# Turning the rows of eight experts in the DMA engines, as 16-bit halves, in place of TensorE

## The reference

```python
scores = jax.nn.softmax(xt @ gate_w.T, axis=-1)
topv, topi = jax.lax.top_k(scores, K)                      # K = 4 of E = 8
topv = topv / jnp.sum(topv, axis=-1, keepdims=True)
g = _silu(jnp.einsum('td,edh->eth', xt, exp_w1))
u = jnp.einsum('td,edh->eth', xt, exp_w3)
yexp = jnp.einsum('eth,ehd->etd', g * u, exp_w2)
routed = jnp.einsum('te,etd->td', combine, yexp)
shared = _silu(xt @ sh_w1) * (xt @ sh_w3) @ sh_w2          # 2048 wide
```

## Time and profile before

| | |
|---|---|
| median of 3 runs | 1568.19 us (1567.37 to 1569.07) |
| the profiled execution, its own time | 1567.0 us |
| its span | 1565.3 us |
| mean granted TensorE clock | 0.999 |
| TensorE busy | 1551.4 us, 99% |
| VectorE busy | 854.2 us, 55% |
| ScalarE busy | 584.7 us, 37% |
| moved by DMA | 205.64 MB, mean 131 GB/s |

### The profile page before, as it was taken

The page is one execution under the profiler, slowest core; times in us unless marked ns, Lnnn a source line. Parts: engine busy times, 40 slices in busy tenths (PEclk is TensorE's granted clock), DMA queues, the critical chain, the costliest instruction groups (busy, mean ns, idle before and its releaser), DMA issues.

```text
span 1565.3 us, 28095 instructions
## 1 busy us (share of the span) xinstructions
PE 1551.4 (99%) x10796; PEld 1534.7 (98%) x10796; DVE 854.2 (55%) x1460; ACT 584.7 (37%) x914; POOL 117.8 (8%) x139
## 2 busy tenths in 40 slices
PE   9999999999999999999999999999999999999998
PEld 9998999999999999999999999999999999999998
DVE  8665569845522344454544545454555366335886
ACT  6332345432222333343444444444444222223442
POOL 1321010000100001000010100001000133001000
PEclk9999999999999999999999999999999999999999
DMA  4412203232422446446464654646555576221333
GB/s 136 133 41 72 76 28 108 82 131 84 123 76 79 157 138 189 151 135 208 137 207 148 191 165 150 202 151 208 161 172 163 160 204 178 83 80 55 94 117 83
DMA packets 71001, 205.64 MB, mean 131 GB/s; under 512 B 13620, under 2 KB 22370, under 8 KB 70890
## 3 DMA queue, kind: packets, MB, share of 16 engines
q1 hardware_dynamic: 45020, 157.94, 32.6%
q0 software_dynamic: 14976, 32.81, 7.0%
q10 hardware_dynamic: 10894, 13.26, 2.7%
HBM read 185.01 MB, written 18.95 MB: 130 GB/s over the span
## 4 chain that ended last, share of the span: by engine, by line
PE 94%; DVE 4%; issue 1%; ACT 1%; ACTq 0%; DVEq 0%; POOL 0%; POOLq 0%
PE acc L1793 86%; PE acc L1773 2%; PE acc L2172 1%; PE acc L2151 1%; DVE w_lo L1277 1%; DVE yrow L1042 0%; PE acc L1842 0%; DVE yrow L1041 0%; ACTq L1000 0%; PE acc L2108 0%; PE acc L1758 0%; PE acc L2225 0%; PE acc L1784 0%; PE acc L1952 0%; DVE acc L1323 0%
## 5 line engine op out<-in xcount | busy, mean ns | idle before, releaser
L1793 PE MATMUL acc<-act_x,w_hi 128*128 128x312 f32 (+8 forms) x2304 | 507.6, 309 | 1.6 <-DVE act_b L1290 0.6
L1793 PE MATMUL acc<-act_b,w_hi 128*128 128x312 f32 (+8 forms) x2048 | 456.0, 311 | 0.0
L1793 PE MATMUL acc<-act_a,w_hi 128*128 128x314 f32 (+1 forms) x1920 | 423.0, 310 | 2.7 <-DVE gath L1349 2.3
L1793 PEld LDWEIGHTS acc<-act_x,w_hi 128*128 128x128 f32 x2304 | 385.3, 188 | 2.5 <-ACT act_a L826 1.0
L1793 PE MATMUL acc<-act_x,w_lo 128*128 128x312 f32 (+8 forms) x1152 | 355.7, 309 | 0.0
L1793 PEld LDWEIGHTS acc<-act_b,w_hi 128*128 128x128 f32 x2048 | 340.2, 189 | 0.1
L1226 DVE TENSOR_TENSOR w_lo<-raw,w_hi 128x1024 fp32r<-128x1024 f32 x253 | 309.0, 1222 | 44.2 <-ACT w_hi L502 43.2
L1793 PEld LDWEIGHTS acc<-act_a,w_hi 128*128 128x128 f32 x1920 | 319.5, 190 | 4.0 <-ACT w_hi L798 2.8
L1793 PE MATMUL acc<-act_b,w_lo 128*128 128x314 f32 (+8 forms) x1024 | 315.6, 308 | 0.0
L1793 PE MATMUL acc<-act_a,w_lo 128*128 128x314 f32 (+1 forms) x960 | 294.9, 307 | 0.0
L502 ACT ACTIVATE w_hi<-raw 128x1024 fp32r<-128x1024 f32 x264 | 277.1, 1051 | 8.3 <-PE acc L1793 4.6
(11 more groups left out here) (239 smaller groups left out, 1247.0 us busy)
## 6 DMA issues: line engine op xcount, KB each, us to landing
raw<-stream_dram SPq DMA_DIRECT2D x296, 512.0 KB, 3.7
y_dram<-yrow POOLq DMA_DIRECT2D x16, 512.0 KB
y_dram<-yrow POOLq DMA_DIRECT2D x8, 352.0 KB
rows<-x_dram ACTq DMA_DIRECT2D x1, 2500.0 KB
x_dram<-rows ACTq DMA_DIRECT2D x5, 500.0 KB
h_rows_dram<-rows ACTq DMA_DIRECT2D x1, 2500.0 KB
rows<-x_dram ACTq DMA_DIRECT2D x8, 312.5 KB
rows<-x_dram SPq DMA_DIRECT2D x5, 448.0 KB
```

What stands on the lines that cost most here:

```text
L1793: ins = pe.matmul(o, w, xs_[h], start=(first and w is hi and xs_ is x_hi), stop=(last and w is lo))
```

## The change

Both turns go from TensorE to the DMA engines, by transposing transfers of 16-bit values. A float32 value is kept as two halves of 16 bits in two separate planes (t = 0 and 1), and each plane is turned by itself. Copies on ScalarE and VectorE take words apart into planes and put planes together to words; they move bits only.

- `h_rows_dram` and `y_dram` hold rows of 2 x 1024 halves. `h_rows` (ScalarE) writes the planes as it copies from PSUM.
- **In:** GpSimd gathers one tile at a time (for the first expert all three, into `rows`); SP turns it by one transposing transfer (`turn_inputs`, three for each expert: 128, 128 and 96 rows of 2048 halves) into `xe_parts`. For experts 1 to 7 the three go through one buffer, `x_stage`: SP issues the turn n of expert r+1 behind the load of unit 11, 15 or 19 of expert r, and GpSimd gathers the next tile when the turn before it has landed. VectorE puts the words of chunk m together in `x32` (`expert_in_word`), in the place where it had copied to `yrow`; the high and low parts are taken from there.
- **Out:** ScalarE copies chunk m from PSUM as planes to `y16` (688 halves in place of 344 words); SP turns it by one transposing transfer (`turn_outputs`, eight for each expert, 128 rows of 768 halves) to `yrow`, ahead of the load of unit m of the next expert (or of `shb`); GpSimd stores when all eight have landed. `y16` has two buffers: the copy of chunk m waits until the turn of chunk m-2 has landed.
- **Back:** the gathered rows land as planes in `act_x`, and ScalarE puts the words together (`back_rows`, 20 copies of 2048 halves), behind each of the first five pairs of `shb`, before VectorE adds them.
- TensorE's functions `expert_in` and `turn_y` are gone, and with them the waits that they held; VectorE's first words of an expert wait for the last up unit, whose inputs they may not overwrite.

The core of the diff (the way for more than 344 tokens in an expert changes likewise):

```diff
-            def gather(e):
+            def gather_list(e):
                 pool.tensor_copy(now_tok[:, :], slot_tok[:, bass.ds(3 * e, 3)]).then_inc(now_ready, 1)
                 pool.wait_ge(h_saved, 16)
                 pool.wait_ge(now_ready, e + 1)
                 pool.sem_inc(gather_go, 1)
-                for n, (c0, cn) in enumerate(SLOT_TILES):
-                    pool.indirect_dma_start(out=grow[0:cn, n, :], out_offset=None, in_=h_rows_dram,
...
+            def gather_rest(e):
+                for n in range(1, 3):
+                    pool.wait_ge(xe_turned, e * (16 * 3) + 16 * n)
+                    pool.sem_inc(gather_go, 1)
+                    gather_tile(x_stage, n)
...
             with pool.Fori(1, EXPERTS - 1) as e:
+                pool.wait_ge(x32_ready, e * KC + KC)
+                gather_list(e + 1)
+                gather_tile(x_stage, 0)
                 save_y(e - 1)
-                pool.wait_ge(xe_tp, e * KC + KC)
-                gather(e + 1)
+                gather_rest(e + 1)
...
+            def turn_inputs(e, n, source, count):
+                c0, cn = X_TILES[n]
+                sp.wait_ge(gathered, 16 * count)
+                if e >= 1 and n == 0:
+                    sp.wait_ge(x32_ready, e * KC)
+                sp.dma_start_transpose(xe_parts[:, :, c0:c0 + cn], source[0:cn, :]).then_inc(xe_turned, 16)
+
+            def turn_outputs(e, m):
+                sp.wait_ge(yt_copied, e * KC + m + 1)
+                if e >= 1 and m == 0:
+                    sp.wait_ge(y_saved, 16 * 3 * e)
+                sp.dma_start_transpose(y_parts[:, :, m * P:(m + 1) * P],
+                                       y16[:, m % 2, :, :].rearrange("p t w -> p (t w)")).then_inc(y_turned[m % 2], 16)
...
+            for r in range(EXPERTS):
+                expert = sp.value_load(order_i[0:1, r:r + 1], min_val=0, max_val=EXPERTS - 1)
+                for j in range(UNITS_EXPERT):
+                    if r >= 1 and j < KC:
+                        turn_outputs(r - 1, j)
+                    load_one(r * UNITS_EXPERT + U_EXP + j, j % RING, expert * UNITS_EXPERT + U_EXP + j)
+                    if j in X_TURNS and r + 1 < EXPERTS:
+                        n = X_TURNS.index(j)
+                        turn_inputs(r + 1, n, x_stage, 3 * (r + 1) + n + 1)
+            for j in range(KC):
+                turn_outputs(EXPERTS - 1, j)
+                load_one(U_SHB + j, j % RING, U_SHB + j)
...
                 for m in range(KC):
                     split_hi(base, UNITS_UP + m + 3)
+                    if nxt:
+                        expert_in_hi(e + 1, m)
                     act.wait_ge(unit_done, base + (UNITS_UP + m + 1))
                     if m >= 2:
-                        act.wait_ge(y_tp, e * KC + (m - 1))
-                    act.activation(prod[:, m % 2, 0:CAP], acc[:, m % 4, 0:CAP], ACT.Copy).then_inc(yt_copied, 1)
-                    if nxt:
-                        expert_in_hi(e + 1, m)
+                        act.wait_ge(y_turned[m % 2], e * (8 * KC) + 16 * (m // 2))
+                    act.activation(y16[:, m % 2, :, 0:CAP],
+                                   acc[:, m % 4, 0:CAP].bitcast(u16).rearrange("p (s t) -> p t s", t=2),
+                                   ACT.Copy).then_inc(yt_copied, 1)
...
+            def back_rows(i):
+                for k in range(TOP):
+                    act.wait_ge(back[k], 16 * (i + 1))
+                    if i >= 1:
+                        act.wait_ge(back_used, TOP * (i - 1) + k + 1)
+                    act.activation(back_slot(k).bitcast(u16).rearrange("p (d t) -> p t d", t=2),
+                                   back_parts[0:TT, k, :, :], ACT.Copy).then_inc(back_words, 1)
+
             for m in range(KC):
                 gated_pair(shb, m, b_hi, None)
+                if m < NT:
+                    back_rows(m)
...
+            def expert_in_word(e, m):
+                if m == 0:
+                    dve.wait_ge(xe_turned, e * (16 * 3) + 16 * 3)
+                if m >= 2:
+                    dve.wait_ge(xe_lo, e * KC + (m - 1))
+                dve.tensor_copy(x32[:, m % 2, :].bitcast(u16).rearrange("p (s t) -> p t s", t=2),
+                                xe_halves[:, :, m, 0:CAP]).then_inc(x32_ready, 1)
...
-                    if m >= 1:
-                        turn_y(e, m - 1)
-                    if nxt:
-                        expert_in(e + 1, m)
```

More of the change, by code:

```diff
@@ L25 @@
 SLOT_TILES = [(0, P), (P, P), (2 * P, CAP - 2 * P)]
+XR = 352
+YC = 3 * P
+X_TILES = [(0, P), (P, P), (2 * P, XR - 2 * P)]
+X_TURNS = (11, 15, 19)
 RING = 4
@@ L81, in build @@
         w_lo = sb("w_lo", [P, RING, D], f32r)
-        silu = sb("silu", [P, TP], f32)
-        prod = sb("prod", [P, 2, TP], f32)
+        work = sb("work", [P, 3 * TP], f32)
         ident = sb("ident", [P, P], f32)
@@ L120, in build @@
         now_tok = sb("now_tok", [P, 3], u32)
+        silu = work[:, 0:TP]
+        prod = work[:, TP:3 * TP].rearrange("p (s w) -> p s w", w=TP)
+        e_silu = work[:, 0:CAP]
+        x32 = work[:, CAP:3 * CAP].rearrange("p (s w) -> p s w", w=CAP)
+        y16 = work[:, 3 * CAP:3 * CAP + 2 * YC].bitcast(u16).rearrange("p (s t w) -> p s t w", s=2, t=2)
+        e_prod = work[:, 3 * CAP:3 * CAP + 2 * YC].rearrange("p (s w) -> p s w", w=YC)
         acc = ctx.enter_context(nc.psum_tensor("acc", [P, 8, 512], f32))
@@ L356, in build @@
         yt_copied = sem("yt_copied")
-        y_tp = sem("y_tp")
-        y_copied = sem("y_copied")
+        y_turned = [sem(f"y_turned{s}") for s in range(2)]
         y_saved = sem("y_saved")
         back = [sem(f"back{s}") for s in range(TOP)]
+        back_words = sem("back_words")
         back_used = sem("back_used")
@@ L440, in _, with load_one @@
             sp.dma_start(bias[:, :, :], biases).then_inc(small_loaded, 16)
+            def load_one(done, s, u):
+                sp.wait_ge(hi_split, done + (1 - RING))
+                sp.wait_ge(lo_split, done + (1 - RING))
+                sp.dma_start(raw[:, s, :], stream[bass.ds(u, 1), :, :].rearrange("u p n -> (u p) n")
+                             ).then_inc(raw_loaded[s], 16)
             def load_four(done, first):
                 for s in range(RING):
[L444 to L448, removed]
+                    load_one(done + s, s, first + s)
             def load_seven(L):
@@ L472, in _ @@
+            for n in range(3):
+                turn_inputs(0, n, rows16[:, n, :, :].rearrange("p t d -> p (t d)"), 3)
+            with sp.Fori((U_SHA + UNITS_UP) // RING, U_EXP // RING) as g:
                 load_four(g * RING, g * RING)
             sp.wait_ge(order_ready, 1)
[L474 to L477, removed]
@@ L1588, in expert @@
                     dve.wait_ge(exp.silu, e * KC + (m + 1))
-                    dve.tensor_tensor(prod[:, m % 2, 0:CAP], acc[:, (2 * m + 1) % 4, 0:CAP], silu[:, 0:CAP],
+                    if prev and m < 2:
+                        dve.wait_ge(y_turned[m], e * (8 * KC))
+                    dve.tensor_tensor(e_prod[:, m % 2, 0:CAP], acc[:, (2 * m + 1) % 4, 0:CAP], e_silu,
                                       ALU.mult).then_inc(exp.prod, 1)
@@ L1611, in add_back @@
                 for k in range(TOP):
-                    dve.wait_ge(back[k], 16 * (i + 1))
+                    dve.wait_ge(back_words, TOP * i + k + 1)
                     w = top_w[0:TT, k, i:i + 1]
@@ L1704, in _ @@
                 chain[:] = main_chain
+            for s in range(2):
+                dve.wait_ge(y_turned[s], EXPERTS * (8 * KC))
             for m in range(KC):
```

151 lines of the change are left out of this document (75 added, 76 removed).

## The result

The changed kernel takes **1544.33 us** (median of 4 runs, 1543.81 to 1547.93), beside 1568.63 us of the kernel before: a ratio of 0.9852, 95% interval 0.9840 to 0.9864. It is 24.3 us faster. 1534 had been forecast, 34.2 us under the 1568.19 that it started from; the time lies inside the forecast's range, at the upper end of its own range (1529 to 1545). The profiled execution is the longest of the four, so the trace shows 3.6 us more than the median does.

What follows compares the result with a forecast made beforehand. TensorE was taken to bound the kernel. 1567.0 - 36.0 (transposes) + 0.5 (`h_rows` planes) + 1.5 (way back) = 1533.0 profiled, 1534 us as median; own range 1529 to 1545, whole range 1529 to 1690.

Steps and rivals of the forecast that it cites:

- The pieces: Turns, high end: source rows cut into 256-byte runs, 11,776 pieces for an expert, 69 us at 171 per us.
- The price of a turn: Transposing transfers in SP's queue: 20 us for an expert, twice the low end of 9.8; high end 69.
- the second sign: SP's turns: one on the way in landing within 6 us (way out: within 4) would confirm the price.
- Rivals 1 and 2: First: SP's queue becomes the bound, 1572 to 1731 us, chance 0.18. Second: pieces turned one after the other, chance 0.10.
- rival 1: SP's queue, loads and turns: gain gone at 48.5 us of turns for an expert, 63 GB/s; chance 0.18.
- Two buffers: Way out: ScalarE's copy waits for the turn two chunks back; costs only from a landing of about 9.7 us on.
- the signs: Expected traces: TensorE some 36 us less busy, no expert gaps; loads landing in 5 to 6 us; ScalarE near 80% in `shb`.
- Six cost 0.57 us, 95 ns each.: TensorE's stream in the experts: price of a transpose; removing 384 gains 36.5 us, taken as 36.0.
- A down unit: 1.22 + 0.52 + 0.92 = 2.7 us of 3.6, hidden.: VectorE in the experts: its split and the copy of 688 halves fit within a unit's 3.6 us, costing nothing.
- I take 1.5 us: Way back in `shb`: cost of ScalarE's 20 copies before the silu TensorE awaits; ends 0 and 8 us.
- The spare of 0.7 us for a pair: Way back in `shb`: four copies, split and silu end at 1283.6, TensorE wants the bank at 1284.34.
- rival 3: Part of the gain given back: turns at 44 to 48 us, or `shb` beyond 8 us; 1546 to 1564; chance 0.06.

Runs made afterwards that it cites:

- e3_both: Changed kernel with VectorE's chunk words ahead of the low part and ScalarE's way-back copies one pair later: 1522.93 us, ratio 0.9710 to the kernel before.
- e4_twice: Changed kernel with second turns of 5 of 6 column blocks out and 5 of 16 in, into unused memory: 1549.24 us, ratio 0.988 to the kernel before.
- e1_words_first: Changed kernel with VectorE making a chunk's words before the next weight's low part in the experts' down units: 1538.29 us, ratio 0.9817 to the kernel before.
- e2_copies_spread: Changed kernel with ScalarE's four way-back copies per tile one pair later, two before and two behind the high part: 1530.68 us, ratio 0.9763.

## Why the forecast was right, and where its steps failed

**Right.** *What bounds the kernel*: TensorE, and with the two orders mended (e3_both) it is busy without a gap again. *The pieces*: 97,024 packets more in the first queue (142,044 against 45,020), 12,128 for an expert: in the trace 11,776 of them have 256 bytes, as counted for the high end, and the others 4. *The price of a turn*: at most 23.5 us of the queue for an expert against 20 taken between ends of 9.8 and 69; landings of 3.6 and 6.6 us, against "within 4 and within 6", so the second sign was missed by 0.6. The argument for it, packets of 4 KB as in a load, did not hold: the pieces were the small ones of the high end, but they moved at 204 GB/s, nearer to the 306 of the low end. That twice the low end came close is in part luck. SP's slack bears it, and by e4_twice 14 us more. Rivals 1 and 2 fall; the pace of the only small pieces in the trace before, 171 per us, was not that of these, some 800 per us. (The 63 GB/s of rival 1 should be 62.) *Two buffers*: landings of 3.6 us in the median never held ScalarE by themselves; L1013 waits for TensorE alone. *ScalarE's chunk copy*: 0.73 us, 0.76 taken. The 0.5 us for the planes of `h_rows` are not resolved: the start of the experts scatters by more.

**Of the signs.** TensorE's busy time fell by 34.4 us (some 36), and the granted clock in the experts fell only behind the gap of 2.06 us. But loads landed in 4.1 us in the median (600 to 1190 us) and not 5 to 6, ScalarE was 61% busy in the first half of `shb` (1193 to 1310 us) and not near 80%, and TensorE waited in the experts too, for the high part of a chunk that VectorE had put together late: a cause that none of the signs named.

**Wrong, three sizes.**

1. *"Six cost 0.57 us, 95 ns each."* The distance to the next product was read, not the next product's own. One row further the answer stood in the trace: the triple behind the group is 0.09 us longer. With 0.66 us for a group of six, 110 ns each, the 384 are worth some 42 us, not 36.5; by the groups as they stand (42 of six, 7 of nine, 23 of three) 43. The doubled transposes agree with the first number, the removed ones with the second: e3_both's experts, 40.8 us shorter for the 357 transposes that stood in them, give 114 ns. This step erred by some 6 us against the change.

2. *"A down unit: 1.22 + 0.52 + 0.92 = 2.7 us of 3.6, hidden."* VectorE's copy was even cheaper, 0.56 us. But sums for each engine do not bound a unit in which two engines wait for one another in turn. The ring is 1.05 + 1.23 + 0.56 + 0.49 + 0.73 = 4.06 us of work, less the overlap of starts: 3.84 measured. Moving two lines of VectorE's order broke it and gave 7.9 us of the stage (e1_words_first). This cost was forecast at nothing.

3. *"I take 1.5 us"* for the way back, ends 0 and 8; it cost 14.9 in the trace. A copy of 2048 halves took 2.4 to 2.5 us, over its upper end of 2.2. The lateness of a gather was named, but priced by one wait of 2.43 us of an engine on which TensorE did not depend; the first gather of the new kernel lands 10 us after ScalarE is ready for it, since it waits for stores that come behind the last turns. The spare of 0.7 us for a pair was right: four copies 0.55 us longer than taken overdraw it by 1.5, and the later gaps are 1.4. Both had been foreseen as kinds, not as sizes, and the fall of the clock behind the gap was not priced at all. This is the condition of rival 3, `shb` beyond 8 us, for which 1546 to 1564 was given; the time stayed under that because the transposes were worth more than forecast.

Together: 36.5 became some 42, given back 7.9 in the experts and 14.9 behind them, so 19 us in the profiled execution, 24.3 by the medians. The profiled execution had been forecast at 1533.0 and took 1547.9, 14.9 us more; the medians differ by 10.3. Without errors of opposite sign, the first some 6 us one way and the other two 21 us the other, the time would lie outside the forecast's own range: that it lies inside is in part luck. Not settled: how the 3.6 us between the profiled execution and the median are spread over the stages.

## What to carry to other kernels

Where two engines hand a piece to and fro, add up the ring, not each engine: an order in which a low part that nobody awaits stands ahead of a copy that somebody does can bind at half load, and swapping two calls frees it. A new wait on an engine that makes what TensorE needs next should stand behind that work, as e2_copies_spread put it; there the same copies cost nothing. For the price of an instruction in a pipelined stream, read the distance to the second instruction behind it too, and double the instruction as well as remove it if the two may differ.

## What the hardware did that was not expected

- Transposing transfers cut into 256-byte pieces moved at 204 GB/s where nothing else moved, some 800 pieces per us, over four times as many as the plain 512-byte ones went, with the DMA engines full. SP's queue was held 1.21 us for 196,608 bytes on the way out, and 4.59 for 524,288 on the way in behind a load, 2.08 without one. The Trainium skill, "DMA: Bandwidth & Descriptors", section "Latency and other measured facts", gives 261 GB/s with a middle dimension that is not contiguous; the trace shows less here.
- A group of transposes in a stream of products cost 0.09 us once, in the products behind it, beside the length of the group itself, whether it had 3, 6, 9, 12 or 18.
- A gap of 9.12 us was followed by 5.7 us of products at a granted clock of 0.50, and one of 2.06 us by 3.4 us at 0.50, which began 1.3 us after the products had gone on. Around one of 1.10 us the clock read 1.00 (1026 to 1036).
- ScalarE's copy of 2048 16-bit values, laid two bytes apart into words, takes 2.4 to 2.5 us, 1.2 ns a value; the copy of 688 out of the banks 0.73 us, and 1024 packed 32-bit values 1.06.
